# The next head's row of shifts: from a bank of the maxima to a bank of the scores

## What is computed

```
x = x + xattn0(layernorm(x), ctx)      # one head of 128
x = x + ffn0(layernorm(x))             # 8 experts, top 1
x = x + xattn1(layernorm(x), ctx)      # 8 heads of 64, scale 1/8, output projection Wo, bo
x = x + ffn1(layernorm(x))             # 32 experts, top 4, one shared
```

## Time and profile before

| | us |
|---|---|
| median of 3 timed runs | 1450.55 |
| lowest and highest of them | 1450.23, 1456.92 |
| the profiled execution | 1452.76 |
| its span, first to last instruction | 1451.0 |
| granted TensorE clock, mean over the span | 0.962 of full |

### The profile page before, as it was taken

One profiled execution on the slowest core, in us unless ns is written; L12 is line 12 of the kernel. 1 busy time (PEld: TensorE's weight loads), 2 busy tenths in 40 slices (PEclk: granted clock), 3 DMA queues, 4 the chain that ended last, 5 costly groups with the idle time before them and its releaser, 6 DMA issues.

```text
span 1451.0 us, 19927 instructions
## 1 busy us (share of the span) xinstructions
PE 1382.4 (95%) x6187; PEld 787.8 (54%) x6187; DVE 1094.6 (75%) x1484; ACT 795.1 (55%) x1578; POOL 941.4 (65%) x542
## 2 busy tenths in 40 slices
PE   5989998887999999999999999999999999998898
PEld 3867775433555555555555555555555455554565
DVE  8976666598877779688777968877796886766555
ACT  3458886323565565556556655655565565453332
POOL 5001113342889889888988888898898899886110
PEclk9999999756999999999999999999999999998799
DMA  6640000400000200200020020002002000000011
GB/s 175 206 129 17 17 17 7 93 2 0 1 1 1 49 1 1 50 1 0 1 49 1 1 50 1 1 1 50 0 1 46 1 1 0 1 1 13 19 40 39
DMA packets 77372, 39.45 MB, mean 27 GB/s; under 512 B 62047, under 2 KB 70000, under 8 KB 77002
## 3 DMA queue, kind: packets, MB, share of 16 engines
q1 hardware_dynamic: 77290, 38.36, 10.6%
HBM read 24.66 MB, written 13.68 MB: 26 GB/s over the span
## 4 chain that ended last, share of the span: by engine, by line
PE 86%; DVE 6%; DMA 3%; ACT 2%; issue 1%; SPq 0%; POOL 0%; ACTq 0%; DVEq 0%; POOLq 0%
PE ps L1392 25%; PE ps L1379 15%; PE ps L1380 13%; PE ps L1345 9%; DMA v_scratch<-v_stage 3%; PE ps L1332 3%; DVE chunk_max L951 2%; PE ps L1536 2%; PE ps L1216 2%; PE ps L1217 2%; PE ps L1218 2%; PE ps L1205 2%; PE ps L1207 2%; PE ps L1206 2%; PE ps L1324 1%
## 5 line engine op out<-in xcount | busy, mean ns | idle before, releaser
L529 POOL TENSOR_TENSOR psums<-psums,probs 126x1024 f32<-126x1024 f32 (+1 forms) x392 | 821.4, 2095 | 122.6 <-ACT probs L713 75.0
L713 ACT ACTIVATE probs<-ps 126x512 f32<-126x512 f32 (+1 forms) x816 | 416.7, 617 | 290.1 <-PE ps L1380 281.5
L951 DVE TENSOR_REDUCE chunk_max<-ps 128x2 f32<-128x1008 f32 (+1 forms) x416 | 472.7, 1180 | 75.7 <-PE ps L1345 74.2
L1392 PE MATMUL ps<-probs,v_mem 126*64 126x512 f32 (+1 forms) x1632 | 389.7, 598 | 0.0
L1379 PE MATMUL ps<-q_heads,ring 128*126 128x512 f32 (+1 forms) x816 | 342.8, 420 | 1.2
L1380 PE MATMUL ps<-q_low,ring 128*126 128x512 f32 (+1 forms) x816 | 322.1, 395 | 0.0
L1002 DVE TENSOR_TENSOR xn<-xn,probs 126x512 f32<-126x512 f32 x126 | 231.9, 1840 | 29.8 <-ACT probs L713 25.6
L678 ACT CAST ring<-ps 64x252 fp32r<-64x252 f32 (+1 forms) x356 | 128.3, 361 | 136.2 <-PE ps L1332 133.1
L1392 PEld LDWEIGHTS ps<-probs,v_mem 126*64 126x64 f32 (+1 forms) x1632 | 111.5, 136 | 165.5 <-issue 121.2
L1379 PEld LDWEIGHTS ps<-q_heads,ring 128*126 128x126 f32 (+1 forms) x816 | 151.9, 186 | 88.5 <-issue 43.9
L1345 PE MATMUL ps<-ring,q_heads 64*128 64x504 f32 (+1 forms) x416 | 170.7, 480 | 17.6 <-DVE chunk_max L951 8.9
(11 more groups left out here) (202 smaller groups left out, 1397.6 us busy)
## 6 DMA issues: line engine op xcount, KB each, us to landing
v_scratch<-v_stage SPq DMA_DIRECT2D x51, 252.0 KB
v_mem<-v_scratch SPq DMA_DIRECT2D x8, 1606.5 KB
ctx_mem<-in_ctx_t SPq DMA_DIRECT2D x3, 803.2 KB, 9.2
vslot<-in_ctx_rows SPq DMA_DIRECT2D x51, 47.2 KB
pair_w<-in_f_pairs SPq DMA_DIRECT2D x17, 128.0 KB, 2.2
pair_w<-in_f_pairs SPq DMA_DIRECT2D x17, 65.0 KB, 1.8
x_tok<-in_x SPq DMA_DIRECT2D x1, 512.0 KB, 4.2
wo<-in_c_wo SPq DMA_DIRECT2D x1, 512.0 KB
```

Of the source, the lines that this page charges most:

```text
L529: pool.tensor_tensor(sums[0:r, 0:width], sums[0:r, 0:width], probs[0:r, n % PROBS, 0:width], ALU.add).then_inc(c_sum, 1)
L713: act.activation(probs[0:r, n % PROBS, cols(half)], ps[0:r, score_bank(t, half), :], ACT.Exp, scale=float(HD) ** -0.5).then_inc(c_exped, 1)
L951: dve.tensor_reduce(chunk_max[:, h % 2, i:i + 2, c], ps[:, banks[0]:banks[1] + 1, 0:group_tiles(c) * KT], AX, ALU.max).then_inc(c_reduced, 1)
L1392: ins = pe.matmul(ps[half * HD:(half + 1) * HD, B_ACC, :], v_tiles[0:r, h % 2, t, :], probs[0:r, n % PROBS, cols(half)], start=(t == 0), s ...
```

## The change

`row_shift` and `shift` take the bank as an argument. For head 0 it is bank 5 as before. For the later heads it is `B_SHIFT` = 1, a bank of the scores. Bank 1 holds, in block 12, the scores of the second half of tile 48; the matmul that turns the shifts now waits until ScalarE has exponentiated these. The second `behind` step, which writes banks 5 and 6, no longer waits for the shifts to be written. The next scores that go to bank 1 are those of the next head's tile 0, second half, and these wait for both halves of the shifts anyway (`c_shift`).

```diff
 B_AUX, B_ACC = 5, 7
+
+B_SHIFT = 1
...
-            def shift(h):
+            def shift(h, bank):
                 dve.wait_ge(c_row, h + 1)
...
-                                      ps[0:TT, B_AUX, 0:P].unsqueeze(1).to_broadcast([TT, tiles, P]),
+                                      ps[0:TT, bank, 0:P].unsqueeze(1).to_broadcast([TT, tiles, P]),
...
-            shift(0)
+            shift(0, B_AUX)
...
                     if b == GROUPS_H - 1 and h + 1 < HEADS:
-                        shift(h + 1)
+                        shift(h + 1, B_SHIFT)
...
-            def row_shift(h):
+            def row_shift(h, bank):
                 pe.wait_ge(c_found, h + 1)
-                pe.matmul(ps[0:TT, B_AUX, 0:P], row_max[:, :], neg_ident[:, :], start=True, stop=True).then_inc(c_row, 1)
+                pe.matmul(ps[0:TT, bank, 0:P], row_max[:, :], neg_ident[:, :], start=True, stop=True).then_inc(c_row, 1)
...
-            row_shift(0)
+            row_shift(0, B_AUX)
...
                             if b == GROUPS_H - 1 and h + 1 < HEADS:
-                                row_shift(h + 1)
+
+                                pe.wait_ge(c_exped, 2 * (TILES * h + b * GT) + B_SHIFT + 1)
+                                row_shift(h + 1, B_SHIFT)
...
                         elif b in (5, 6) and h + 2 < HEADS:
                             pe.wait_ge(c_qlo, 2 * (h + 2) + b - 4)
-                        elif b == GROUPS_H - 1 and h + 1 < HEADS:
-                            pe.wait_ge(c_shift, 2 * h + 4)
                         max_scores(step, PAIRS[k])
```

## The result

| | before | after |
|---|---|---|
| median of 20 runs each, us | 1454.52 | 1449.43 |
| lowest and highest, us | 1450.23, 1457.07 | 1447.04, 1454.65 |
| ratio, 95% interval | | 0.9971, 0.9962 to 0.998 |
| profiled execution, us | 1452.76 | 1454.65 |
| span, us | 1451.0 | 1452.9 |

The kernel is 0.3% faster: 4.2 us by the ratio and 5.1 us between the medians, where 4.6 us were forecast. The absolute time of 1449.43 us lies 3.4 us above the forecast of 1446.0 and 0.2 us above the upper end of the range, 1449.2. The profiled execution of after happens to be the slowest of its 20.

The account below looks back on a forecast made before the run. TensorE's queue, busy 95% of the span, was taken to bound the kernel. Six boundaries at 0.76 us give 4.6 us, so 1450.55 - 4.6 = 1446.0 us, 0.3% less; range 1443.9 to 1449.2.

Parts of the forecast that it names:

- The removed wait: Last blocks of heads 0 to 5: second `behind` step starts 0.94 us earlier, the next TensorE work 1.03 us earlier.
- TensorE's gain on arrival: At each of six boundaries, weights times values start 1.03 us earlier, before any new wait on VectorE.
- VectorE is late next: Bank 3's weight load then waits on VectorE's chain through `k_lo`: 0.23 to 0.31 us lost, 0.72 to 0.80 kept per boundary.
- The added wait and the bank: Turn of the shifts waits for bank 1's exponentials, 1.1 us margin; shifts unchanged in the new bank: cost taken as zero.
- All kept: VectorE's chain has more air, so 6 x 1.03 = 6.2 us go, giving 1444.4 us; chance 0.18.
- Given back in the next head: GpSimd 0.17 us late in the next head, or VectorE twice in the way: 2 to 4.6 us return, about 1449; chance 0.13.
- The slower rival: GpSimd's sum starts first, delaying VectorE's reductions and `k_lo` by 2.08 us: 8.2 us lost, 1458.7 us; chance 0.07.
- the last one of the sum: Subtracts the 4.6 us gain from the timed runs' median, 1450.55 us, to forecast 1446.0 us.

Follow-up runs that it names:

- The loaded kernels: One more VectorE reduction (0.66 us) between `behind` reductions and `k_lo`; first to seventh turn 755.17 us on the kernel before, 754.40 us on the changed kernel.
- the relieved one: Changed kernel with VectorE's sum of tile 47 in block 12 moved ahead of the shifts: 749.04 us first to seventh turn, ratio to before 0.9958.
- its counterpart without the change: Kernel before with only VectorE's sum of tile 47 moved ahead of the shifts: 755.28 us first to seventh turn.
- the large reduction: Changed kernel with a VectorE reduction of 512 fp32 per partition between the shifts and VectorE's sum of tile 47: 774.37 us first to seventh turn.

## Why the prediction was right in the change and wrong in the time

- **The removed wait.** It was the last one at the six boundaries and gives all of the gain: with the wait put back, 755.22 us. TensorE's gain on arrival, forecast 1.03 us, is 1.06 us. That a head is as long as TensorE's queue, from which the forecast sets out, stands in the earlier trace rows.
- **VectorE is late next.** `k_lo` starts without waiting, and the load for bank 3 stands idle for 0.55 us (forecast about 0.5). A boundary keeps (755.30 - 751.00) / 6 = 0.72 us, or 4.3 us in all; I had 0.72 to 0.80 and took 0.76, or 4.6 us. The loaded kernels, the relieved one and its counterpart without the change show that it is VectorE, and that it is late only once the wait is gone. The lower value is what the trace shows at this place: `k_lo` starts 0.03 us behind the end of the reduction. The overlap of 0.08 us, from which the higher one came, was read where VectorE's sum follows the shifts, and was not to be carried over to `k_lo`. The kernel before could have decided between the two. In 28 places between its turns `k_lo` follows a reduction without waiting for anything else, and it never starts before the reduction's end (505.38 + 2.31 = 507.69 here):

```profile
505.38 2.31 DVE L951 TENSOR_REDUCE chunk_max<-ps 128x2 f32<-128x1008 f32 x2
507.72 0.85 DVE L941 TENSOR_TENSOR ring<-ps,ring 64x252 fp32r<-64x252 f32 x2
```

- **The added wait and the bank** cost nothing that shows, as forecast.
- **All kept** was false here, and true with 0.6 us less on VectorE.
- **Given back in the next head** was false: the intervals from turn to turn are 125.77, 125.77, 125.66, 125.98, 125.74 and 122.08 us, each 0.66 to 0.76 us shorter than before.
- **The slower rival** did not happen, and the long sum that it is about exists (2.75 to 2.81 us with the large reduction). VectorE's sum does start as GpSimd changes, within 0.1 us of the end of GpSimd's sum at all six boundaries, but a delay of 0.2 us does not yet lose its place. I had underpriced the case itself, at 1.36 us a boundary more than before. With the large reduction it was (774.37 - 755.30) / 6 = 3.18 us, of which the reduction itself is 0.6 us. I had left out the first `before` step and the clock.
- **The step that failed is the last one of the sum**: "against that it is 1450.55 - 4.6 = 1446.0 us". The base was the median of three runs. Two were 0.3 us apart, and I took that distance for the scatter, though the third lay 6.4 us higher. The same kernel's median over 20 runs is 1454.52 us, and over 20 and 11 others 1455.23 and 1454.63 us. Less 4.6 us, the first gives 1449.9 us, and 1449.43 us were measured. The draw was bad luck: of the 51 executions of this kernel in the three series only three are below 1451 us, and two of them were in my three. The range that took no account of it was my error. The profiled execution, at 1452.76 us, had said that the base could be higher; I put the whole 2.2 us down to the profile. Where the clocks are on record, the time goes with them, and the lost clock lies outside the stretch between the turns. That the three runs were fast for this reason is not shown, since their clocks were not recorded; and what makes a run fall into one pattern or another was not tried.
- The profiled execution of after was forecast at 1448.2 us by way of before's 1452.76. It came out at 1454.65, at a clock of 0.955. At 0.962, that of before, the two runs of after are at 1448.76 us on average.

## What to carry to other kernels

Removing the last wait of a place is worth only the distance to the next one: lay out each engine's chain behind the wait, and the smaller of the two slacks is the gain; then look for work of the engine that is late next that fits in the idle time it has ahead of the wait. Compare spans between two events inside the stretch that the change touches, because here these repeat within 0.1 us while whole runs scatter by 8 to 10. And take the base of a forecast in absolute time from many runs, or give the range the scatter of the whole kernel and not that of two runs that happened to agree.

## What the runs showed of the hardware

- On one core, with the same program, most of the spread from run to run (10.5 us before, 7.6 us after) goes with the mean granted clock: 0.98 and 0.69 us for each 0.001, with correlations of -0.90 and -0.92.
- The granted clock stood at 1.00 or at 0.50 in every profile. With the large reduction ahead of VectorE's sum, where TensorE's weight loads were idle for 2.67 to 2.74 us and its matmuls for 1.78 to 1.86 us at a boundary, a stretch of 3.4 us at 0.50 followed at each of the six; with 1.09 to 1.11 and 0.77 to 0.79 us, as in the kernel before, none did.
- VectorE's sum of two operands in SBUF takes 0.67 to 0.69 us when it starts ahead of GpSimd's sum or, by the rows, up to 0.03 us behind it, and GpSimd's sum is then longer (up to 2.92 in place of 2.37 us). It takes 2.75 to 2.81 us when it starts 0.11 to 0.41 us behind.
- Between two of its sums GpSimd was mostly idle for 0.14 us, and for 0.44 us at the first boundary. The 0.44 us stand there also in the run with the large reduction, where VectorE's sum came too late to use them: GpSimd ended at 473.32 and began at 473.76, VectorE's sum began at 473.87.
- VectorE's low part of the keys never overlapped the reduction ahead of it (it started 0.03 to 0.05 us behind its end, 28 times in the kernel before), while a reduction behind a reduction started 0.07 to 0.09 us before the end of the first (155 times there).
